# Weight chunks of a quantised FFN spread over more attention passes, and the FFN's tiles reordered on VectorE and ScalarE

## The reference, cut to what matters

```
x = x + tanh(g_xattn[0]) * L0_xattn(layernorm(x), ctx_512, ...)
x = x + tanh(g_ffn[0])   * L0_ffn(layernorm(x), w_gate, w_up, w_down)
x = x + tanh(g_xattn[1]) * L1_xattn(layernorm(x), ctx_512, ...)
x = x + tanh(g_ffn[1])   * L1_moe(layernorm(x), ...)

def quant_weight(w):                  # per matrix
    scale = mean(abs(w)) + 1e-5
    return clip(round(w / scale), -1, 1), scale
def quant_act(x):                     # per row
    s = max(abs(x), axis=-1) / 127 + 1e-5
    return clip(round(x / s), -128, 127), s
def qlinear(x, w):
    (wq, ws), (xq, xs) = quant_weight(w), quant_act(x)
    return (xq @ wq.T) * xs * ws
L0_ffn = qlinear(silu(qlinear(x, w_gate)) * qlinear(x, w_up), w_down)   # hidden width 2048
```

## Time and profile before

| | |
|---|---|
| three runs | 2138.41, 2132.03, 2133.57 us, median 2133.57 |
| the profiled execution's own time | 2135.03 us |
| its span, first to last instruction | 2133.3 us |
| mean granted TensorE clock | 0.951 of full |
| busy in the span: PE, DVE, ACT, POOL | 88%, 66%, 45%, 32% |
| latent attention, end of its last output product (L547) on PE | 1087.3 us |
| FFN, first L1088 to last addition | 1103.1 to 1330.9 us |

### The profile page before, as it was taken

The page is one execution under the profiler, slowest core; times in us unless marked ns, Lnnn a source line. Parts: engine busy times, 40 slices in busy tenths (PEclk is TensorE's granted clock), DMA queues, the critical chain, the costliest instruction groups (busy, mean ns, idle before and its releaser), DMA issues. The chain is left out here.

```text
span 2133.3 us, 31242 instructions
## 1 busy us (share of the span) xinstructions
PE 1870.0 (88%) x11258; PEld 1465.9 (69%) x11258; DVE 1414.6 (66%) x2782; ACT 950.9 (45%) x2029; POOL 676.3 (32%) x628
## 2 busy tenths in 40 slices
PE   4899999999889888988967857899867889999997
PEld 4677777777677667766744423566545789999996
DVE  5776776777777876778666675477654535666664
ACT  3444444444434433443333322555424236666664
POOL 4323212225412231223110130232221464665653
PEclk9999999999999999999989988799978999999999
DMA  4022221120112332121060000000013247777774
GB/s 193 16 81 79 80 78 38 49 79 31 51 57 81 125 103 76 40 87 51 1 250 24 30 24 31 18 2 1 1 56 119 84 100 204 236 237 235 234 235 91
DMA packets 52397, 192.38 MB, mean 90 GB/s; under 512 B 7678, under 2 KB 11902, under 8 KB 41494
## 3 DMA queue, kind: packets, MB, share of 16 engines
q1 hardware_dynamic: 40550, 167.01, 22.1%
q0 software_dynamic: 11408, 23.37, 5.8%
q10 hardware_dynamic: 288, 0.00, 0.0%
HBM read 156.99 MB, written 33.36 MB: 89 GB/s over the span
## 5 line engine op out<-in xcount | busy, mean ns | idle before, releaser
L359 POOL TENSOR_TENSOR la_q_roped<-la_q_roped 128x400 f32<-128x400 f32 x128 | 136.2, 1085 | 698.4 <-DVE la_q_roped L808 698.3
L713 ACT ACTIVATE la_probs<-banks,la_minus_max 100x361 f32<-100x361 f32 x256 | 144.4, 564 | 195.6 <-DVE la_minus_max L901 195.6
L808 DVE TENSOR_TENSOR la_q_roped<-banks,la_rope_q 128x400 f32<-128x400 f32 x384 | 197.4, 566 | 19.6 <-PE banks L469 9.8
L2041 DVE TENSOR_TENSOR ex_weights_low<-ex_raw_weights,ex_weights_high 128x2048 fp32r<-128x2048 f32 x60 | 137.6, 2293 | 52.3 <-ACT ex_weights_high L1936 51.9
L523 PEld LDWEIGHTS banks<-identity,la_probs 100*121 100x121 f32 x768 | 113.4, 185 | 71.3 <-DVE la_probs L908 48.9
L908 DVE TENSOR_SCALAR la_probs<-la_probs,la_rsum 100x361 f32<-100x361 f32 x256 | 149.3, 583 | 9.1
L901 DVE TENSOR_REDUCE la_minus_max<-banks 100x1 f32<-100x361 f32 x256 | 135.1, 528 | 25.9 <-PE banks L514 19.3
L534 PE MATMUL banks<-la_probs_t,la_kv_rows 121*128 121x200 f32 x768 | 151.4, 333 | 0.0
L1088 PE MATMUL banks<-qf_sign_weights,qf_x_quant_t 128*128 128x512 bf16 (+1 forms) x416 | 106.1, 408 | 50.5 <-DVE qf_hidden L1217 48.4
L523 PE MATMUL banks<-identity,la_probs 100*121 100x100 f32 x768 | 126.5, 273 | 21.6 <-DVE la_probs L908 18.4
L2308 POOL TENSOR_TENSOR ex_g_low<-ex_g,ex_g_high 128x256 fp32r<-128x256 f32 (+1 forms) x104 | 86.6, 949 | 181.4 <-ACT ex_g_high L1980 181.0
(11 more groups left out here) (334 smaller groups left out, 5308.2 us busy)
## 6 DMA issues: line engine op xcount, KB each, us to landing
ex_raw_weights<-w_exp SPq DMA_DIRECT2D x60, 1024.0 KB, 5.1
la_weights<-w_pack SPq DMA_DIRECT2D x15, 1856.0 KB, 7.6
la_kv_turned<-w_ffn SPq DMA_DIRECT2D x30, 384.0 KB, 3.3
la_rope_k<-w_ffn SPq DMA_DIRECT2D x30, 384.0 KB, 3.4
qf_sign_weights<-ffn_signs SPq DMA_DIRECT2D x3, 2048.0 KB, 13.8
ffn_signs<-la_ffn_signs SPq DMA_DIRECT2D x30, 192.0 KB, 2.1
residual<-x SPq DMA_DIRECT2D x2, 2048.0 KB, 14.7
out<-ex_block_out POOLq DMA_DIRECT2D x13, 256.0 KB, 4.3
```

Source lines behind the costliest of these rows:

```text
L359: pool.tensor_tensor(roped[:, h, 0, c, :], roped[:, h, 0, c, :], roped[:, h, 1, 1 - c, :], ALU.add).then_inc(b_add, 1)
L713: act.activation(prob[:, s % 4, 0:L], ps[0:S, s % 2, 0:L], ACT.Exp, bias=nmax[:, s % 4:s % 4 + 1], accum_out=sums[:, s % 4:s % 4 + 1]).the ...
L808: dve.tensor_tensor(roped[:, h, v, c, :].rearrange("p (b s) -> p b s", b=GB), ps[:, B_BANKS[k % 2], 0:NT].rearrange("p (b s) -> p b s", b=GB),
L2041: dve.tensor_tensor(wl[:, m, :], raw[:, m, :], wh[:, m, :].bitcast(F32), ALU.subtract).then_inc(w_low[m], 1)
```

## The change

**In the attention** the sign chunks go five to a pass, over passes 9 to 15: three in the front and two in the slots near the end of the same pass (scaled by ScalarE in slots 16 and 18, clipped and stored by DVE in slots 18 and 20). Pass 15 has three, in its front. ScalarE's second chunk of a front moves behind `high(n, 2)`, and DVE's third from behind `low(n, 3)` to behind `rope(n, 2, 1)`. On the SP queue the last two chunks' stores and loads stand ahead of the next weight load, and the first three behind it, so that a pass's weights are no longer loaded behind all chunks of the pass before; the store of the first residual half moves ahead of the first sign chunk.

**In the FFN** DVE takes a maximum behind each block of 512 columns (new tile `qf_h_part_max`), and `h_scales` combines the four; ScalarE does the first rounding pass (`scaled`, over 2048 columns, behind its fourth block); `add` stands behind the scales and ahead of the second rounding pass; `x_quantise` moves between the first two blocks of the next tile, and the bn_stats behind the second.

```diff
-        FIRST_SUM, FIRST_SIGN, EACH = 1, PAIRS + 1, 6
+        FIRST_SUM, EACH_SUM, FIRST_SIGN, EACH_SIGN = 1, 6, PAIRS + 1, 5
+        SCALE_AT, SIGN_AT = (ITEMS, ITEMS + 2), (ITEMS + 2, ITEMS + 4)
...
                 for n in range(2, RUNS + 1):
                     refill_sums(n - 1)
-                    refill_signs(n - 1)
+                    refill_signs(n - 2, slice(3, None))
                     if n == RUNS:
+                        refill_signs(n - 1, slice(0, None))
                         continue
...
                     if n == PAIRS + 1:
                         load_chunk(0)
                         load_chunk(1)
+                    refill_signs(n - 1, slice(0, 3))
...
                 def pair(n):
+                    summing = len(chunks_of(n, False)) > 0
                     chunk(n, 0)
-                    chunk(n, 1)
+                    if summing:
+                        chunk(n, 1)
                     high(n, 2)
-                    chunk(n, 2)
+                    chunk(n, 2 if summing else 1)
                     high(n, 3)
...
+                    else:
+                        chunk(n, 2)
...
+                        if s in SCALE_AT and not summing:
+                            chunk(n, 3 + SCALE_AT.index(s))
...
                     low(n, 3)
-                    chunk(n, 2)
...
                     rope(n, 2, 0)
-                    chunk(n, 3)
                     rope(n, 2, 1)
-                    chunk(n, 4)
+                    chunk(n, 2)
...
                     rope(n, 2, 2)
-                    chunk(n, 5)
...
+                        if s in SIGN_AT:
+                            chunk(n, 3 + SIGN_AT.index(s))
...
+                def scaled(t):
+                    n, par = rows_of_tile(t), t % 2
+                    act.wait_ge(h_small, t * 3 + 2)
+                    act.activation(h[0:n, par, :], h[0:n, par, :], ACT.Identity, bias=rnd[0:n, 0:1],
+                                   scale=hinv[0:n, par:par + 1]).then_inc(h_mul, 1)
...
                     widen(t, NC - 1)
+                    scaled(t)
...
+                    dve.wait_ge(u_out, t * NC + c + 1)
+                    dve.tensor_reduce(hpart[0:n, par, c:c + 1], h[0:n, par, cs], AX.X, ALU.max,
+                                      apply_absolute_value=True).then_inc(h_part, 1)
...
-                    dve.wait_ge(h_small, t * 3 + 3)
-                    dve.tensor_scalar(h[0:n, par, :], h[0:n, par, :], hinv[0:n, k], ROUND,
-                                      ALU.mult, ALU.add).then_inc(h_mul, 1)
+
+                def h_quantise(t):
+                    n, par = rows_of_tile(t), t % 2
                     dve.wait_ge(h_mul, t + 1)
...
                 for t in range(PT):
-                    widen(t)
+                    dve.wait_ge(scales, 2 * t + 2)
+                    for c in range(NC):
+                        widen(t, c)
+                        if c == 0 and FIRST <= t + FIRST - 1 < PT:
+                            if t:
+                                x_quantise(t + FIRST - 1)
+                        if c == 1:
+                            for g, steps in enumerate(((7, 8), (11, 12))):
+                                if t - 1 in steps:
+                                    batch_stats(g, steps.index(t - 1))
+                    h_scales(t)
                     if t + FIRST < PT:
                         x_scales(t + FIRST)
                     if t:
                         add(t - 1)
-                    quantise(t)
-                    if t + FIRST < PT:
-                        x_quantise(t + FIRST)
...
+                    h_quantise(t)
+                batch_stats(1, 1)
                 add(PT - 1)
```

More of the change, by code:

```diff
@@ L242, in latent_attention, with chunks_of @@
         KV_BANKS = (T_BANK, V_BANK)
-        def chunks_of(n, first):
-            return range(max(0, (n - first) * EACH), max(0, min(len(chunks), (n - first + 1) * EACH)))
+        def chunks_of(n, again):
+            first, each = (FIRST_SIGN, EACH_SIGN) if again else (FIRST_SUM, EACH_SUM)
+            return range(max(0, (n - first) * each), max(0, min(len(chunks), (n - first + 1) * each)))
         def loads_of(c, again):
@@ L300, in refill_sums, with refill_signs @@
                             load_chunk(c + 2)
-                    if n == FIRST_SUM + -(-len(chunks) // EACH) - 1:
+                    if n == FIRST_SUM + -(-len(chunks) // EACH_SUM) - 1:
                         sp.wait_ge(q_abs, len(chunks))
                         sp.dma_start(trigk_all[:], rope_k).then_inc(tab_k, 16)
-                def refill_signs(n):
-                    for c in chunks_of(n, FIRST_SIGN):
+                def refill_signs(n, which):
+                    for c in chunks_of(n, True)[which]:
                         m, lo, width = chunks[c]
@@ L669, in chunk @@
                 def chunk(n, k):
-                    for first, again in ((FIRST_SUM, False), (FIRST_SIGN, True)):
-                        if k >= len(chunks_of(n, first)):
+                    for again in (False, True):
+                        if k >= len(chunks_of(n, again)):
                             continue
-                        c = chunks_of(n, first)[k]
+                        c = chunks_of(n, again)[k]
                         m, lo, width = chunks[c]
@@ L1248, in add, with batch_stats @@
                                              in1=x, op0=ALU.mult, op1=ALU.add).then_inc(o_add, 1)
+                def batch_stats(g, half):
+                    dve.wait_ge(core.rows_in[g], 16 * GB)
+                    for b in range(2):
+                        b += g * GB + 2 * half
+                        dve.bn_stats(core.stats[:, b, :], core.x[:, b, :]).then_inc(n_bn, 1)
                 lo = core.packed[1][0]
```

45 lines of the change are left out of this document (20 added, 25 removed).

## The result

The changed kernel takes 2048.47 us (median of 4, 2045.38 to 2053.51), the kernel before 2133.83 on the same chip; the ratio is 0.9599 with a 95% interval of [0.9573, 0.9625]. 2053.4 was predicted, in a range of 2038 to 2082, with 0.95 on faster. The profiled execution is the slowest of the four, 2053.51 us with a span of 2051.8, against 2135.03 and 2133.3 before. The 81.5 us between the two spans lie so: the first exponential of the last pass comes 24.9 us earlier (1023.4, was 1048.3), the FFN is 57.5 us shorter (1078.07 to 1248.41, 170.3 us; was 227.8), and the stages behind it are 1.0 longer.

The account below looks back on a forecast made before the run. TensorE bounds attention passes, with chunks costing extra; in the FFN, TensorE waits for VectorE's chain each fast tile. From 2135.03 us, 26.3 (attention) and 55.3 (FFN) come off: 2053.4 us, range 2038 to 2082.

Parts of the forecast that it names:

- The layout: One FFN tile laid out in time from TensorE's start of the down product: wait covered, 0.75 us to spare, 11.65 us a tile.
- the rows' 0.44: FFN tile, VectorE: four maxima cost 0.44 us more than one by the profile's rows; the forecast used this.
- the estimate of 0.18: FFN tile, VectorE: four maxima cost 0.18 us more than one, estimated from the Trainium skill's 58-cycle fixed cost.
- the split: FFN tile 8: GpSimd's split holds VectorE's rounding passes, adding 5.0 us, between 2 and 12.
- the end: FFN's end, from the last tile's T0 through second pass, transposes, product and addition: 14.7 us, before 18.1.
- The mis-sized term: Attention front: three chunks cost 2.9 us, 2.2 for two plus 0.7 for the third; bounds 2.2 and 4.4.
- the SP queue's new order: Attention, SP queue: weights loaded behind the signs of slot 20, still earlier than before, so no cost was counted.
- the prediction's upper bound: Attention: at most 30.5 us saved, with fronts at 2.2 us each; 26.3 was forecast, 17.3 the lower bound.
- Rival 1: FFN tile: GpSimd's hold brings TensorE's wait and clock alternation back, 13.5 us a tile, 2073 us in all; chance 0.18.
- Rival 2: Attention: chunks cost the same anywhere, nothing saved there, 2079.7 us; chance 0.12, with or without the FFN hold.
- Rival 3: FFN: VectorE's chain to the next first multiplication stays the period; 2108.7 us with all 55.3 lost; chance 0.04.
- Rival 4: FFN: TensorE, busy without a break, gets the lower clock throughout; 23.3 us a tile, 2181 us; chance 0.02.

Follow-up runs that it names:

- the four ablations: Four kernels, each undoing or delaying one part of the changed kernel's FFN tile order: 2049.68 (delay), 2063.31, 2064.16 and 2066.31 us.
- weights_first2: Changed kernel with the loads of weights and packed rows ahead of the pass-end chunks' signs on the SP queue: 2042.9 us, ratio 0.9573 to the kernel before.
- the three ablations: Three kernels, each undoing one part of the changed kernel's FFN tile order: 2063.31, 2064.16 and 2066.31 us.
- five_in_front: Changed kernel with all five chunks of a pass in the front, none at its end: 2086.93 us (one run).
- two_in_front: Against weights_first2, one more chunk moved from the front to the pass's end, two in front and three at the end: 2049.32 us, ratio 0.9607 to the kernel before.
- dve_rounds: Changed kernel with the first rounding pass back on VectorE, behind the addition: 2063.31 us, period 12.21 us against 11.48.
- one_max: Changed kernel with one maximum over 2048 columns instead of four of 512: 2064.16 us, period 12.50 us against 11.48.
- add_first: Changed kernel with the addition ahead of the scales, as in the order before: 2066.31 us, period 12.99 us against 11.48.
- The repeated run: The changed kernel run again without edits: 2048.32 us, ratio 0.9608 to the kernel before.

## Why the prediction was right, and where it was off

- **FFN, the tile.** 11.65 us was taken from before's busy time; it is 11.48. The layout put the fourth multiplication's end at 1.7 (1.66), ScalarE's pass at 2.9 to 5.0 (3.0 to 5.1), the next multiplication at 7.05 (7.33, by the hold of 0.32), and TensorE's want at 7.8 (7.71, from the four ablations). So 0.4 us was to spare where 0.75 had been reckoned. It was enough. The instructions' prices stood: 0.69 for a maximum, 2.09 for ScalarE's pass. Four maxima take 2.76 us where the one took 2.28, 0.48 more: the rows' 0.44 was near, the estimate of 0.18 was not.
- **FFN, the rest.** T0 of tile 1 came 1.6 us nearer to the first gate row (1.5 predicted), the split cost 16.13 - 11.48 = 4.65 (5.0), the end took 14.69 (14.7): 57.5 us saved against 55.3, and most of the difference is 0.17 a tile.
- **Attention.** 24.9 us saved against 26.3. The mis-sized term is the front: 2.9 predicted for three chunks, 2.3 measured in an ordinary pass and nothing for the third; pass 14 takes 65.1 where 66.6 stood, which was not looked into. Against it stands a step that failed: the SP queue's new order was costed at nothing because the weights' load is still early enough for its own user. The price fell on who stands behind it: chunk 0's signs, 4.6 us in pass 10 and up to 2.6 in pass 13. The store's wait by name was not in the prediction. Without these two, in `weights_first2`, passes 9 to 15 take 443.1 us against 475.1 before: 32.0 saved, more than the 30.5 of the prediction's upper bound. The waits for transfers went nearly as said: ScalarE waits 8.2 us in all for `w_ffn` in passes 9 to 15, 3.4 of them in the front of pass 10, where it waited 7.5 in one pass before.
- **Rival 1** was half right: the hold exists in every tile with x work, 0.32 us where 0.5 was feared, and there was no wait to pay. Its second half, that a wait just above the spare time brings the clock's alternation, is refuted by the three ablations. The Trainium skill's rule that GpSimd and VectorE's two-port instructions block each other ("Advanced Engine Details and Errata", VectorE Performance Modes) agrees with both holds, 0.32 us in each tile and 3.1 in tile 8.
- **Rival 2** is refuted by `five_in_front` and bounded by `two_in_front`: two chunks are hidden at the end, a third isn't (0.9 us). **Rival 3** is what `dve_rounds`, `one_max` and `add_first` become, by 0.7 to 1.5 us a tile: any one of the three edits left out brings the wait back. **Rival 4** is out: the clock is 1.00 over seven tiles without a break.
- **The total.** The profiled execution is 0.1 us from the forecast, but the median lies 4.9 below. That nearness is luck. The attention saved 1.4 us less than forecast and the FFN 2.2 more; and within the attention, fronts that were cheaper by about 6 us made up for most of the 7 us that the SP queue's order cost. The repeated run's profile (span 2044.8) shows what varies: it reached pass 7's first exponential at 496.4 us instead of 500.5, and its FFN's end took 13.07 us instead of 14.69, with a granted clock of 0.87 instead of 0.77. The last one was among the prediction's bounds.

## What to carry to other kernels

Lay one period out in time, with the instant at which the bounding engine wants its operand; what an edit is worth is what it moves across that instant, and the engines' sums of busy time can point the other way. When a transfer's issue is moved in a queue, price those behind it, a single buffer's store above all, and not only its own user. Background work goes into the slots where the engines wait anyway; measure how many such slots there are, since the first item beyond them already costs time.
